# Shared hidden units computed turned: weights standing, 512 tokens streaming

## The reference

```
x = x + attention(layernorm(x), ctx, ctx, lens)
t = layernorm(x) as 1024 rows of 256
probs = softmax(t @ Wg);  eidx = argmax;  gate = probs[eidx]
pos   = place of the token among those of its expert, in order of tokens
keep  = pos < 128
routed: h = silu(xd @ W1[e]) * (xd @ W3[e]);  oe = h @ W2[e]   (8 experts, 128 rows each, 352 units)
shared = (silu(t @ sw1) * (t @ sw3)) @ sw2                     (all 1024 rows, 352 units)
x = x + gate * keep * oe[place of the token] + shared
```

## Time and profile before

| what | value |
| --- | --- |
| median of 3 runs | 159.94 us (159.8 to 160.06) |
| the profiled execution | 160.61 us |
| its span in the profile | 158.8 us |
| PE busy | 146.4 us, 92% of the span |
| DVE, ACT, POOL busy | 101.9, 86.5, 62.9 us |
| mean granted TensorE clock | 0.989 |

### The profile page before, as it was taken

The page is one execution under the profiler, slowest core; times in us unless marked ns, Lnnn a source line. Parts: engine busy times, 40 slices in busy tenths (PEclk is TensorE's granted clock), DMA queues, the critical chain, the costliest instruction groups (busy, mean ns, idle before and its releaser), DMA issues.

```text
span 158.8 us, 3537 instructions
## 1 busy us (share of the span) xinstructions
PE 146.4 (92%) x1291; PEld 102.7 (65%) x1291; DVE 101.9 (64%) x250; ACT 86.5 (55%) x197; POOL 62.9 (40%) x88
## 2 busy tenths in 40 slices
PE   7779999998999999999999998997899999999940
PEld 2445565454555545554555787995799989999820
DVE  0499786689687887875232546677866677776220
ACT  3443265755748575656767198345583386663300
POOL 7115839304607150321010000066598077827550
PEclk9999999999999999999999999999999999999995
DMA  3992534453160700000350878012238712212110
GB/s 81 336 360 70 165 114 132 148 172 107 30 246 11 261 1 5 0 6 0 102 177 2 272 257 287 9 41 93 74 101 221 258 39 84 74 55 91 64 60 33
DMA packets 15824, 18.42 MB, mean 116 GB/s; under 512 B 1980, under 2 KB 15077, under 8 KB 15808
## 3 DMA queue, kind: packets, MB, share of 16 engines
q1 hardware_dynamic: 14368, 14.98, 29.7%
q0 software_dynamic: 1152, 2.97, 5.5%
q10 hardware_dynamic: 288, 0.26, 0.5%
HBM read 14.12 MB, written 4.21 MB: 115 GB/s over the span
## 4 chain that ended last, share of the span: by engine, by line
PE 77%; DVE 7%; ACT 5%; issue 5%; DMA 2%; POOL 1%; SPq 0%; POOLq 0%; DVEq 0%
PE bank L982 17%; PE bank L1019 11%; PE bank L1003 9%; PE bank L1217 5%; PE bank L1157 4%; PE bank L1192 4%; PE bank L1193 4%; PE bank L1071 4%; PE bank L1069 4%; PE bank L934 3%; DMA xs<-in_x 2%; PE bank L1031 2%; PE bank L1046 2%; PE bank L1039 2%; DVE nm L524 2%
## 5 line engine op out<-in xcount | busy, mean ns | idle before, releaser
L524 DVE TENSOR_REDUCE nm<-bank 128x2 f32<-128x512 f32 x64 | 40.9, 685 | 11.2 <-PE bank L982 11.2
L773 ACT ACTIVATE pt<-bank 128x512 f32<-128x512 f32 x64 | 34.5, 589 | 15.8 <-PE bank L1003 15.6
L1003 PE MATMUL bank<-qz,kz 32*128 32x256 f32 x256 | 40.9, 402 | 0.0
L982 PE MATMUL bank<-kz,qz 32*128 32x256 f32 x256 | 35.1, 403 | 0.9 <-DVE qz L502 0.9
L982 PEld LDWEIGHTS bank<-kz,qz 32*128 32x128 f32 x256 | 21.9, 184 | 13.3 <-issue 7.7
L1003 PEld LDWEIGHTS bank<-qz,kz 32*128 32x128 f32 x256 | 24.9, 184 | 4.5 <-ACT pt L773 2.8
L1019 PE MATMUL bank<-pt,vext 128*32 128x256 f32 x256 | 20.2, 391 | 0.0
L437 POOL DMA_INDIRECT expert_rows<-rk,idx_s x8 | 8.0, 1002 | 24.2 <-DVE rk L612 20.6
L373 POOL TENSOR_SCALAR qz<-xs,rs,mrs 128x256 f32<-128x256 f32 x14 | 7.7, 562 | 20.9 <-DVE mrs L496 20.9
L398 POOL TENSOR_SCALAR mrs<-mv,rstd 128x1 f32<-128x1 f32 x6 | 1.6, 260 | 30.5 <-ACT rstd L785 30.5
L464 POOL DMA_INDIRECT vext<-out,rk x8 | 9.7, 1215 | 7.1 <-DMA out<-xs 5.0
(11 more groups left out here) (164 smaller groups left out, 316.9 us busy)
## 6 DMA issues: line engine op xcount, KB each, us to landing
wraw<-in_w SPq DMA_DIRECT2D x10, 352.0 KB, 3.4
wraw<-in_w SPq DMA_DIRECT2D x10, 128.0 KB, 3.4
expert_rows<-zero SPq DMA_DIRECT2D x1, 1032.0 KB, 5.7
out<-xs SPq DMA_DIRECT2D x8, 128.0 KB, 3.1
xs<-in_x SPq DMA_DIRECT2D x3, 256.0 KB, 5.9
cs<-in_ctx SPq DMA_DIRECT2D x3, 256.0 KB, 6.1
wraw<-in_sw SPq DMA_DIRECT2D x2, 352.0 KB, 5.7
kz<-in_w SPq DMA_DIRECT2D x2, 352.0 KB, 4.0
```

Of the source, the lines that this page charges most:

```text
L524: nc.vector.tensor_reduce(nm[:, b % 2, :, place], scores_bank[:].rearrange("p (u c) -> p u c", u=2), AX_X, ALU.max, negate=True).then_inc( ...
L773: nc.scalar.activation(pt[:, g % NPT, n % 4, :], sc_bank[n % NS][:], ACT.Exp).then_inc(exped, 1)
L982: mm = nc.tensor.matmul(scores_bank[:, u * D:(u + 1) * D], qz[rows, b, half, u * P:(u + 1) * P], kz[rows, b, half, :], start=True, stop=True)
L1003: mm = nc.tensor.matmul(sc_bank[n % NS][:, c * D:(c + 1) * D], kz[rows, b, half, c * P:(c + 1) * P], qz[rows, b, half, :], start=True, sto ...
```

## The change

Eight blocks of tokens become two halves of four blocks, and the 352 units become three pieces of 128, 128 and 96. A unit of work is one piece for one half (`UPS`, six in all, the 96-row piece first in each half). Now the **weights stand** (a piece of `shi` or `slo`, with the 8 router columns beside the 96 units) and **512 tokens stream**, so a result has units on partitions and 512 tokens along the row. It is already turned for the down product. Logits come out as 8 rows of 512 tokens; ACT copies them to a small tile and PE turns them back with four matmuls of 8 columns per half. Routing has two parts of four blocks. The low parts of the first half move from DVE to POOL, ahead of the scatters. The last block's attention output uses another bank. The last weighed values stand between the first two pieces of the ups. Stores of the first four blocks go to SP ahead of the reads of expert rows. Memory is laid out anew: `late` holds silu results, products and logits, `wlate` the weights of experts 5 to 7, and results go to `xs`.

```diff
-WEIGH = [(2 * m + LAG + 3, 2 * m + LAG + 4) for m in range(NG)]
+WEIGH = [(2 * m + LAG + 3, 2 * m + LAG + 4) for m in range(NG - 1)] + [(END, END)]
-ROUTED = ((0, 3), (3, 6), (6, B))
+ROUTED = ((0, 4), (4, B))
+HALF = B // 2
+UPS = ((0, 2), (0, 0), (0, 1), (1, 2), (1, 0), (1, 1))
+ROWS_OF = (P, P, FL)
...
+            for b in range(HALF):
+                store_base(b)
             sp.wait_ge(xd_sent, 16 * B)
...
+            pool.wait_ge(x2_made, B - 2)
+            for k in range(3):
+                shared_low(k)
             send_rows(0)
+            expert_low(0, 0)
             send_rows(1)
-            send_rows(2)
-            expert_low(0, 0)
             expert_low(0, 1)
-            expert_low(1, 0)
-            expert_low(1, 1)
+            for e in (1, 3):
+                expert_low(e, 0)
+                expert_low(e, 1)
...
+            def shared_hidden(k):
+                rows = ROWS_OF[UPS[k][1]]
+                dve.wait_ge(silu_done, k + 1)
+                nc.vector.tensor_tensor(sig[k % 3][0:rows], u3_bank[k % 3][0:rows, :], sig[k % 3][0:rows],
+                                        ALU.mult).then_inc(h_made, 1)
...
+            def shared_silu(k):
+                rows = ROWS_OF[UPS[k][1]]
+                act.wait_ge(up_done, k + 1)
+                if k >= 3:
+                    act.wait_ge(h_lo_pool, k - 2)
+                nc.scalar.activation(sig[k % 3][0:rows], u1_bank[k % 3][0:rows, :], ACT.Silu).then_inc(silu_done, 1)
+
+            def shared_logits(half):
+                act.wait_ge(up_done, UPS.index((half, 2)) + 1)
...
+                nc.scalar.copy(lgt[FL:FL + E], u1_bank[0][FL:FL + E, :]).then_inc(lg_copied, 1)
+
+            def shared_high(k):
...
+                act.wait_ge(h_made, k + 1)
+                nc.scalar.copy(hThi[0:rows, half, f], sig[k % 3][0:rows]).then_inc(h_hi, 1)
...
             def shared_up(k, c):
+                half, f = UPS[k]
                 if c == 0:
+                    pe.wait_ge(x_lo, HALF * (half + 1))
...
+                    if k >= 3:
+                        pe.wait_ge(h_made, k - 2)
...
+                        nc.tensor.matmul(u1, weights(part, S1 + f * P, F + WG, c, n1), tokens, start=a, stop=z)
+                        mm = nc.tensor.matmul(u3, weights(part, S3 + f * P, F, c, n3), tokens, start=a, stop=z)
...
+            for b in range(B):
                 shared_down(b)
-                if b + 2 < B:
-                    turn_hidden(b + 2)
-                if b == B - 2:
-                    turn_rows(0)
+            pe.wait_ge(route, routed(len(ROUTED) - 1, "cum"))
+            for _ in range(4):
+                nc.tensor.matmul(counts[:].rearrange("p (n c) -> p n c", c=P), onesb[:],
+                                 onesb[:].unsqueeze(1).broadcast_to([P, 4, P]), start=True, stop=True)
+            turn_rows(0)
             turn_rows(1)
```

More of the change, by code:

```diff
@@ L356, in _ @@
                 sp.dma_start(xe[:, a:z, :], xd[:, a:z, :]).then_inc(ld_xe[i], 16)
-            for b in range(B):
-                sp.wait_ge(shared_added, b + 1)
-                sp.dma_start(out[b], xs[:, b, :]).then_inc(base_stored, 16)
+            for b in range(HALF, B):
+                store_base(b)
         @block.gpsimd
@@ L544, in add_attention @@
                 dve.wait_ge(o_back, b + 1)
-                nc.vector.tensor_tensor(xs[:, b, :], back, xs[:, b, :], ALU.add).then_inc(added, 1)
+                nc.vector.tensor_tensor(xs[:, b, :], back if b < B - 1 else last_back, xs[:, b, :],
+                                        ALU.add).then_inc(added, 1)
             def token_stats(b):
@@ L723, in _ @@
                     rows_low(e + 2)
-                    if e >= 1:
+                    if e >= 2:
                         expert_low(e + 2, 0)
@@ L1066, in shared_up @@
+                n1, n3 = ROWS_OF[f] + (WG if f == 2 else 0), ROWS_OF[f]
+                u1, u3 = (of[k % 3][0:n, :].rearrange("p (b t) -> p b t", b=HALF)
+                          for of, n in ((u1_bank, n1), (u3_bank, n3)))
                 for xpart, parts in ((xhi, (shi, slo)), (xlo, (shi,))):
+                    tokens = xpart[:, HALF * half:HALF * (half + 1), c, :]
                     for part in parts:
                         a, z = (c == 0 and xpart is xhi and part is shi), (c == DC - 1 and xpart is xlo)
-                        nc.tensor.matmul(u1, xpart[:, b, c, :], weights(part, S1, F + WG, c, F + WG), start=a, stop=z,
-                                         skip_group_check=True)
@@ L1071, in shared_up, with turn_logits @@
-                        mm = nc.tensor.matmul(u3, xpart[:, b, c, :], weights(part, S3, F, c, F), start=a, stop=z,
-                                              skip_group_check=True)
+                        nc.tensor.matmul(u1, weights(part, S1 + f * P, F + WG, c, n1), tokens, start=a, stop=z)
+                        mm = nc.tensor.matmul(u3, weights(part, S3 + f * P, F, c, n3), tokens, start=a, stop=z)
                 if c == DC - 1:
                     mm.then_inc(up_done, 1)
+            def turn_logits(half):
+                pe.wait_ge(lg_copied, half + 1)
+                if half == 0:
+                    pe.wait_ge(x_lo, B - 1)
+                for b in range(HALF):
+                    mm = nc.tensor.matmul(logits[:, HALF * half + b, :], lgt[3 * ROWS:P, b * P:(b + 1) * P],
+                                          cst[3 * ROWS:P, IDENT + 3 * ROWS:IDENT + 3 * ROWS + E], start=True,
+                                          stop=True)
+                mm.then_inc(lg_turned, 1)
@@ L1097, in _ @@
                     shared_up(0, 1)
-                for m in range(NG):
+                for m in range(NG - 1):
                     for c in range(2):
@@ L1154, in shared_down @@
                 k = 0
-                for c in range(FC):
+                for f in range(FC):
+                    rows = ROWS_OF[f]
                     for hpart, part in ((hThi, shi), (hThi, slo), (hTlo, shi)):
-                        mm = nc.tensor.matmul(y_bank[b % 2][:, 0:D], hpart[:, b % 2, c * P:(c + 1) * P],
-                                              weights(part, S2, D, c, D), start=(k == 0), stop=(k == 3 * FC - 1))
+                        mm = nc.tensor.matmul(base_bank[b % 2][:, 0:D], hpart[0:rows, half, f, j * P:(j + 1) * P],
+                                              part[0:rows, S2 + f * D:S2 + (f + 1) * D],
+                                              start=(k == 0), stop=(k == 3 * FC - 1))
                         k += 1
@@ L1191, in expert_up @@
                         lhs = rows[:, c * P:(c + 1) * P]
-                        nc.tensor.matmul(u1_bank[e % 2][:, 0:F], lhs, weights(part, W1, F, c, F), start=a, stop=z)
-                        mm = nc.tensor.matmul(u3_bank[e % 2][:, 0:F], lhs, weights(part, W3, F, c, F),
+                        nc.tensor.matmul(eu1_bank[e % 2][:, 0:F], lhs, weights(part, W1, F, c, F), start=a, stop=z)
+                        mm = nc.tensor.matmul(eu3_bank[e % 2][:, 0:F], lhs, weights(part, W3, F, c, F),
                                               start=a, stop=z)
```

332 lines of the change are left out of this document (157 added, 175 removed).

## The result

The changed kernel takes **176.35 us** in the median of 4 runs (176.02 to 176.74); the kernel before took 159.87 beside it (159.78 to 160.06). The ratio is 1.1018, with a 95% interval of 1.0995 to 1.1041. The forecast was 162.1, its range 160.8 to 164.2: right in sign, wrong by 14 us.

A forecast was written before the change was run, and what follows sets the result against it. PE's queue was taken as the bound, so expert 0's start decides: 124.2 against 121.9 is +2.3, less 0.1 in the expert stage, +2.2. Against the median of 159.94 that gives 162.1 us, range 160.8 to 164.2.

The forecast's parts named there:

- The first wait: PE before the second half's ups, idle 1.9 us until DVE's product 0, starting again at 100.67.
- the table load: ACT loads the silu table only after the scale, 97.37 + 1.28 = 98.65, ahead of silu 0.
- The second wait: PE before the logits of half 1, idle 1.9 us until ACT's copy at 107.0.
- a half unit: Six up matmuls of 512 columns on PE: 6 x 0.227 + 0.08 = 1.44 us.
- the logits: Turning logits back on PE, 0.32 us a half, 0.6 in all.
- Between nothing and a transpose (0.11) each: Price bounds for each of 8 matmuls of 8 columns turning logits back; 0.08 us taken.
- POOL and DVE get in each other's way: Rival: DVE's low 4 waits up to the rest of POOL's instruction, 0.9 us; time 163.0, chance 0.12.
- Low part 4: DVE's subtraction in the shared stage, placed inside POOL's subtraction from 111.5 to 113.2; there the rival put its 0.9 us.
- down 2: PE waits here for DVE's first add, 1.2 us idle, and starts at 115.38.
- a rounding copy and a subtraction move, worth about 0.1 us: Claim that the expert stage stays almost as it is, gaining about 0.1 us at its start.
- The clock: Rival: a PE wait of up to 1.9 us makes the clock fall; 164 to 166 us, chance 0.05.
- The last scatter: POOL's eighth scatter ends at 117.96, following low parts done at 106.36; rows are back at 122.5.

The follow-up runs named there:

- experiment 9: The changed kernel with idle matmuls on PE in its waits (11 and 12 in the first two, 28 before down 2, 64 before down 6); 177.13 us.
- experiment 7: The changed kernel, with POOL waiting for the end of each of its expert subtractions before starting the next; 169.22 us.
- experiment 2: The changed kernel, with POOL issuing all eight scatters before its first subtraction for expert 0; 175.61 us.
- experiments 6: The changed kernel, scatters first, POOL making expert 2's low parts instead of expert 3's, logits turned by four transposes a half; 165.38 us.
- experiment 8: The changed kernel with idle matmuls on PE, 26 before down 2 and 76 before down 4, the latter block misplaced; 180.35 us.

## Why the prediction was wrong

*Up to 112 us it held.* The shared stage began at 87.86. The first wait was 1.56 us (1.9 forecast), and it ended at 101.49 with DVE's product, as forecast: the product's row ends at 101.39. (The column of waits names the low part of the last tokens, which ended at 100.79; PE's list waits for both.) What led there was not the table load, though, but PE itself, which turned the last tokens at 99.55 and not 98.60. The second wait was 1.73 (1.9), on ACT's copy of the logits; it ended at 107.81 (107.0). Silu 593 ns, rounding copies 620, product 690, POOL's low part 1284: within 5% of the prices taken. Two terms were short: a half unit took 1.48 us in the mean of the twelve, not 1.44 (0.2325 a matmul, and some 0.1 at its start where it follows other work), and the logits 0.98 a half, not 0.32; the first 0.66 of that is most of PE's lateness at 99.55, the second came on top behind the second wait. "Between nothing and a transpose (0.11) each" was asked of the wrong number, four a half instead of eight, and each took 0.12. Together they put the downs at 113.40 instead of 111.88: **1.5 us**.

*The step that failed is the rival "POOL and DVE get in each other's way"*, its price and its place. It had the mechanism and a chance of 0.12. Its price went up to "the rest of POOL's instruction, 0.9", and it was laid on low part 4. Low part 4 was not the one; the index instruction was, 2.23 us longer than alone, and it put down 2 at 119.04, **3.66 us** after the forecast (1.5 of them carried over). And the two subtractions for expert 2 that the change moves among the adds I had counted at nothing in this stage ("a rounding copy and a subtraction move, worth about 0.1 us"). They face POOL's own five in a row, so the price is the whole rest of POOL's run. From down 2 to the end of the downs I had 6.6 us, and the chain has 16.4: **9.8 us**, of which the hold with its adds is 6.0 above the two downs that it hides, and the two falls of the clock 3.9 as the chain shows them (by experiment 9 only 1.5 would be saved without them, because the first hides under the hold). The rest of the way to expert 0 was 0.2 shorter. The sum is 1.5 + 2.1 + 9.8 - 0.2 = 13.2 of the 13.3 between 124.2 and 137.47. The last 1 us of the miss lies in the step from the profiled execution to the median: the forecast was 162.8 for the one and 162.1 for the other, and 176.02 and 176.35 came.

*The trace before was silent here.* I had seen that DVE's subtractions from SBUF ran after POOL's in the trace before and never beside them. In that trace DVE began them at 122.92, 0.45 us behind POOL's end at 122.47, so it could not tell. I took the silence of the trace for a small number instead of asking which of the moved instructions would meet POOL's 6.70 us for the first time.

The Trainium skill has the rule in GPSIMD Engine Reference, section 8 "Key points", which I cited, and more fully in SBUF — State Buffer, section "Who interferes with whom", which I had not weighed: whoever starts first has the shared pair of SBUF ports for the whole instruction and the other stands still, for a DVE instruction with two SBUF inputs beside a POOL instruction that reads SBUF, and also for `tensor_scalar` when it runs in a two-port mode. The second part fits as well, though no trace names the mode: the `tensor_scalar` that makes `gate` on 128x4 took 0.73 us beside POOL's low part and 0.17 alone, `past` 1.12 in experiment 7. In one point the measurement goes further than the page: the loser stood still to the end of runs of four, five and six POOL instructions (5.12, 7.43, 10.81 us), and in experiment 2 it was DVE that had the earlier recorded start, by 0.23 us. By the page alone, for one POOL instruction, the hold would have been 1.7 us at most; only the whole run taken as one gives the 7 us.

*The clock*, a rival of its own at 0.05, came as a consequence. In the profiled run it was not one of the waits of up to 1.9 us that I had named, but those of 3.3 and 5.3 us that the holds made. The traces of experiments 6, 7 and 8 show that the shorter ones can do it too, in some executions. For one fall I had priced two to four us of work at the low level; no row showed that. Behind the two holds PE worked 5.8 and 3.7 us at it.

*The last scatter*, forecast to end at 117.96, ended at 122.06. Of this 1.8 us are POOL's wait for the gates that stood behind the held index. Another 2.0 are a step that I had wrong: I let the first scatter go when POOL's low parts were done (106.36), but it waited for the first part's gates and began at 108.38. It cost nothing on top: PE was later still.

## What to carry to other kernels

Before an instruction with two SBUF inputs is moved on DVE, look at what POOL does at that time, and price it by the end of POOL's whole unbroken run, not by one instruction. Leave a gap in POOL's list (a wait on its own last result was enough in experiment 7), or move the work to the other engine, if something on the path stands behind it on DVE. When a new tiling comes out slower, read first the few instructions in the chain whose duration differs from that of their own form elsewhere; here taking the holds of two of 227 on DVE away gave back 10.5 of the 16.5 us, and with the lists put right the tiling was even.

## What the runs showed of the hardware that I had not expected

- A DVE instruction with two SBUF inputs took 10.81 us beside six POOL subtractions in a row, and 0.88 alone. A small one is held as well: on 128x4 numbers one took 2.39 us, and 0.16 alone.
- The POOL instruction that holds it need not have begun by its record: DVE's index began 0.63 us before the recorded start of POOL's subtraction and was held, and without that subtraction in the queue it was not.
- POOL's subtractions were not slowed by any of this while its list had no gap (4.99 us for three, 1.66 each). With gaps they were (6.34).
- The granted clock fell in some executions and not in others, behind waits of 1.6 and 1.7 us: the list of PE is the same up to there in the changed kernel (1.00 from 110 to 112 us), in experiment 7 (0.50) and in experiment 8 (0.56).
- Eight fp32 records of 8 columns took 0.98 us, four transposes of 32 columns 0.36.
